# A two-layer attention kernel: moving bulk loads, small loads and a bias network to other steps

## The reference, cut to what matters

```
xn   = layernorm(x) * g_in
q    = xn @ Wq          (512 -> 16 heads x 64);   k, v = xn @ Wkv (one k and one v, shared by all heads)
k, v = a "null" key and value put ahead of the 128 keys and values
sim  = q k^T (scaled) + bias per head, causal mask, mask per item
out  = softmax(sim) v  @ Wo   (1024 -> 512)
x    = x + layernorm(out) * g_out
```

## Time and profile before

| what | us |
|---|---|
| median of 3 runs | 1381.46 |
| the three runs | 1381.04, 1381.46, 1384.83 |
| the profiled execution's own time | 1385.04 |
| its span | 1383.2 |
| PE busy in the span | 1290.3 |
| DVE, ACT, POOL busy | 1108.7, 859.8, 748.5 |
| mean granted TensorE clock | 0.973 of full speed |

### The profile page before, as it was taken

One profiled execution on the slowest core, in us unless ns is written; L12 is line 12 of the kernel. 1 busy time (PEld: TensorE's weight loads), 2 busy tenths in 40 slices (PEclk: granted clock), 3 DMA queues, 4 the chain that ended last, 5 costly groups with the idle time before them and its releaser, 6 DMA issues.

```text
span 1383.2 us, 28922 instructions
## 1 busy us (share of the span) xinstructions
PE 1290.3 (93%) x8152; PEld 1189.2 (86%) x8152; DVE 1108.7 (80%) x2968; ACT 859.8 (62%) x3245; POOL 748.5 (54%) x1337
## 2 busy tenths in 40 slices
PE   3675599999999999999989999999999999999997
PEld 3564499999999999999988899999999999999996
DVE  5573477778777877787789989999899999999886
ACT  3443366666666666666676666666666666666663
POOL 3341244444444444444446666766676667766773
PEclk8788799999999999999999999999999999999999
DMA  9106501110111111110101101110111011101101
GB/s 282 28 8 105 154 27 41 45 45 30 38 45 45 32 36 45 45 38 31 46 26 45 47 28 41 45 45 24 44 45 45 23 45 45 45 23 45 45 31 39
DMA packets 44723, 67.46 MB, mean 49 GB/s; under 512 B 8160, under 2 KB 16352, under 8 KB 44688
## 3 DMA queue, kind: packets, MB, share of 16 engines
q1 hardware_dynamic: 43056, 66.93, 16.0%
q0 software_dynamic: 288, 0.10, 0.2%
q10 hardware_dynamic: 1344, 0.02, 0.1%
HBM read 48.16 MB, written 18.87 MB: 48 GB/s over the span
## 4 chain that ended last, share of the span: by engine, by line
PE 85%; DVE 5%; SPq 4%; POOL 2%; issue 2%; ACT 1%; DMA 1%; POOLq 0%; DVEq 0%; ACTq 0%
PE bank_q L1187 27%; PE bank_y L1319 24%; PE bank_s L1187 11%; PE bank_o L1187 10%; PE bank_p L1286 6%; PE bank_t L1259 4%; PE bank_t L1227 2%; SPq L327 1%; SPq L379 1%; DMA p_sb<-in_L_cond_g 1%; PE bank_t L1264 1%; DVE wo_l L841 0%; DVE wq_l L832 0%; DVE qt_l L984 0%; DVE wq_raw L869 0%
## 5 line engine op out<-in xcount | busy, mean ns | idle before, releaser
L702 ACT ACTIVATE p_raw<-s_sb,neg_m 128x130 f32<-128x130 f32 (+1 forms) x1024 | 371.9, 366 | 144.4 <-DVE neg_m L1042 141.2
L555 POOL TENSOR_TENSOR p_sb<-p_raw,rden 128x256 f32<-128x256 f32 x256 | 157.1, 614 | 396.3 <-DVE rden L1048 396.3
L1187 PE MATMUL bank_q<-wq_h,xt_h 128*128 128x384 f32 x768 | 270.0, 352 | 7.4 <-DVE xt_l L940 7.2
L1187 PE MATMUL bank_q<-wq_h,xt_l 128*128 128x384 f32 x768 | 261.5, 340 | 0.0
L1187 PE MATMUL bank_q<-wq_l,xt_h 128*128 128x384 f32 x768 | 261.0, 340 | 0.0
L545 POOL TENSOR_TENSOR bias_g<-bias,mask_row 128x260 f32<-128x260 f32 x256 | 177.9, 695 | 125.1 <-DVE s_sb L1035 123.1
L1319 PE MATMUL bank_y<-wo_h,ot_h 128*128 128x512 f32 x512 | 218.8, 427 | 0.3 <-DVE ot_l L1058 0.3
L1319 PE MATMUL bank_y<-wo_h,ot_l 128*128 128x512 f32 x512 | 203.2, 397 | 0.0
L1319 PE MATMUL bank_y<-wo_l,ot_h 128*128 128x512 f32 x512 | 202.9, 396 | 0.0
L702 ACT ACTIVATION_READ_ACCUMULATOR p_raw<-s_sb,neg_m 128x1 f32 x1024 | 193.1, 189 | 0.0
L1035 DVE TENSOR_TENSOR s_sb<-bank_s,bias_g 128x392 f32<-128x392 f32 x256 | 143.0, 559 | 43.4 <-PE bank_s L1187 43.4
(11 more groups left out here) (124 smaller groups left out, 3113.1 us busy)
## 6 DMA issues: line engine op xcount, KB each, us to landing
x_in<-in_x SPq DMA_DIRECT2D x32, 256.0 KB, 2.7
x_res<-in_x SPq DMA_DIRECT2D x32, 256.0 KB, 2.7
x_mid<-y_out SPq DMA_DIRECT2D x32, 256.0 KB, 2.0
x_in<-x_mid SPq DMA_DIRECT2D x32, 256.0 KB, 2.7
x_res<-x_mid SPq DMA_DIRECT2D x32, 256.0 KB, 2.7
out_x<-y_out SPq DMA_DIRECT2D x32, 256.0 KB, 2.0
wq_raw<-in_L_cond_Wq SPq DMA_DIRECT2D x4, 768.0 KB, 14.2
wo_raw<-in_L_cond_Wo SPq DMA_DIRECT2D x1, 2048.0 KB, 12.9
```

The costliest lines, as they stand in the source:

```text
L555: e.tensor_tensor(to[:, 0:2 * P].rearrange("p (e j) -> p e j", e=2), low_blocks(of)[:, :, 2:LOW], r[:, 0:2, :].broadcast_to([P, 2, P]), AL ...
L702: last = e.activation(p_raw[:, g % 2, lo:hi], s_sb[:, g % 2, lo:hi], ACT.Exp, bias=neg_m[:, h:h + 1], accum_out=esum[:, h:h + 1])
L1187: last = e.matmul(out, a, b, start=(k == 0), stop=(k == len(passes) - 1))
```

## The change

In words: the loads for layer 1 leave `between(2)` and go, one group per step, into SP's step behind the load of `x_in`: the table store in step 3, Wq and Wkv in step 29, the bias reads in step 30, Wo in step 31. SP's start is put in another order (network rows ahead of the bias, the bias in two halves around `x_in` (0,1), the mask after it); the three null loads go to ACT's queue. The other small loads, with the null bias and `g_in` of layer 1 among them, are issued by POOL early (12 DMAs), followed by both `place_nulls`. ACT does one tiny exponential first. `output_weights(0, 1)` moves to step 0 on POOL and, on ACT, from behind `exps(3)` to behind `exps(2)`. On DVE and ACT the first `split_qt` stages stand ahead of the network's norm and silu. The second silu's quarters 2 and 3, the second transposes and the table move one step on (the table to the start of step 3). `net` and `net_t` move into `wq_raw`. The loops begin at item 4 instead of 3.

```
-FIRST, LAST = 3, B - 4
+FIRST, LAST = 4, B - 4
...
-        net = y_out[:, 0, :]
-        net_t = y_out[:, 1, :].rearrange("p (c t) -> p c t", c=KC)
+        net = wq_raw[:, 2, 0:D]
+        net_t = wq_raw[:, 3, 0:D].rearrange("p (c t) -> p c t", c=KC)
...
# SP
                     load_x(m)
+                if (m := at(0)) is not None:
+                    bulk(m)
...
-            def between(n):
-                if n == 2:
+            def bulk(m):
+                if is_item(m, 0, 3):
                     e.wait_ge(net_step, TABLE)
                     e.dma_start(table, table_sb.unsqueeze(1).broadcast_to([H, P, 2 * P])).then_inc(table_stored, 16)
+                if is_item(m, 0, B - 3):
                     load_wq(1)
+                if is_item(m, 0, B - 2):
+                    e.wait_ge(table_stored, 16)
+                    load_bias1()
+                if is_item(m, 0, B - 1):
                     for half in range(2):
                         e.wait_ge(wo_ready[half], 1)
                     load_wo(1)
-                    e.wait_ge(table_stored, 16)
-                    load_bias1()

             load_x((0, 0))
             load_wq(0)
-            for half in range(2):
-                rows = slice(half * DH, (half + 1) * DH)
-                null(null_k_col[rows, :], cond[0:1, :].rearrange("a d -> d a"))
-            null(null_v[:, :], cond[1:2, :].broadcast_to([P, DH]))
-            load_bias0()
-            load_mask(0)
+            for dst, src in ((w0_b, w0[0]), (b0_b, b0), (g_b[0], g0)):
+                net_row(dst, src)
+            load_bias0(0)
             wait(e, xn_ready, (0, 0))
             load_x((0, 1))
-            for dst, src in ((w0_b, w0[0]), (b0_b, b0), (g_b[0], g0)):
-                net_row(dst, src)
+            load_bias0(1)
+            load_mask(0)
             load_wo(0)
...
# POOL
+            def start_output(m):
+                if is_item(m, 0, 0):
+                    output_weights(0, 1)
             def between(n):
                 if n == 1:
-                    output_weights(0, 1)
                     net_deviation(VE2)
+                if n == 2:
                     null_norm()
-                    place_nulls(1)
...
                 on(0, normalise, 2)
+                on(0, start_output)
                 on(0, normalise, 3)
...
-            never_seen()
             causal_masks()
             inverse_deviations(item_of(-3))
+            load_small()
+            never_seen()
+            e.wait_ge(null_bias_loaded, 16 * LAYERS)
+            place_nulls(0)
+            place_nulls(1)
             mask_bias0()
             inverse_deviations(item_of(-2))
+            masked_bias((0, 0), 1)
             net_deviation(VE1)
-            e.wait_ge(null_bias_loaded, 16 * LAYERS)
-            place_nulls(0)
-            for g in (1, 0, 2):
-                masked_bias((0, 0), g)
-            load_small()
+            masked_bias((0, 0), 0)
+            masked_bias((0, 0), 2)
...
# ACT: g_in of layer 1 and the null bias go to POOL's load_small
+            load_g_in(0)
+            for half in range(2):
+                rows = slice(half * DH, (half + 1) * DH)
+                e.dma_start(null_k_col[rows, :], cond[0:1, :].rearrange("a d -> d a")).then_inc(nulls_loaded, 16)
+            e.dma_start(null_v[:, :], cond[1:2, :].broadcast_to([P, DH])).then_inc(nulls_loaded, 16)
+            e.wait_ge(consts_ready, 4)
+            e.activation(esum[:, 0:1], minus_half[:, 0:1], ACT.Exp).then_inc(act_warm, 1)
+            e.wait_ge(act_warm, 1)
...
                 on(0, exps, 2)
+                on(0, start_output, 1)
...
                 on(0, exps, 3)
-                on(0, start_output, 1)
...
-                on(1, start_copy, 2, TP2, TCOPY2)
+                on(0, start_copy, 2, TP2, TCOPY2)
...
-            net_silu(GAIN1, EXP1)
             split_qt(first, 0)
             split_qt(first, 1)
+            net_silu(GAIN1, EXP1)
...
# DVE
-                on(0, net_second_silu, [2])
...
                 on(1, split_kt)
-                on(0, net_second_silu, [3])
+                on(-1, net_second_silu, [2, 3])
...
-                if n == 2:
+                if n == 3:
                     second_null()
...
+            q_scale_out(first, 2)
             ln_apply(second)
-            q_scale_out(first, 2)
+            split_qt(first, 0)
             net_norm(RSTD1, CEN1, g_b[0])
-            split_qt(first, 0)
+            split_qt(first, 1)
             net_silu(EXP1, PLUS1, REC1, [0])
-            split_qt(first, 1)
-            net_silu(EXP1, PLUS1, REC1, [1])
             split_kt(first)
             x_stats(third)
             means_variances(item_of(-1))
-            net_silu(EXP1, PLUS1, REC1, [2, 3])
+            net_silu(EXP1, PLUS1, REC1, [1, 2, 3])
...
# PE: second transposes at item 2 instead of 1, table at item 3 instead of 2 (on DVE too)
```

More of the change, by code:

```diff
@@ L249, in build @@
         null_scaled = sem("null_scaled")
+        act_warm = sem("act_warm")
         null_col = sem("null_col")
@@ L356, in low_and_up, with load_bias0 @@
                 return low, up
-            def load_bias0():
+            def load_bias0(pair):
                 heads = bias0.rearrange("(g r e) i j -> r i g e j", g=G, r=2)
-                for pair in range(2):
-                    low, up = low_and_up(0, pair)
-                    for k in range(2):
-                        e.dma_start(low[:, :, k, :], heads[pair, HALF:P, :, k, :]).then_inc(bias0_loaded, 16)
-                        e.dma_start(up[:, :, k, :], heads[pair, 0:HALF, :, k, 0:HALF]).then_inc(bias0_loaded, 16)
+                low, up = low_and_up(0, pair)
+                for k in range(2):
+                    e.dma_start(low[:, :, k, :], heads[pair, HALF:P, :, k, :]).then_inc(bias0_loaded, 16)
+                    e.dma_start(up[:, :, k, :], heads[pair, 0:HALF, :, k, 0:HALF]).then_inc(bias0_loaded, 16)
             def load_mask(layer):
@@ L429, in _ @@
             load_mask(1)
-            stream(e, step, between)
+            stream(e, step)
             e.wait_ge(x_stored, 16 * N)
@@ L448, in load_small @@
             def load_small():
+                for layer in range(LAYERS):
+                    e.dma_start(null_bias_sb[:, layer, :], row(null_bias[layer]).broadcast_to([P, H]))\
+                        .then_inc(null_bias_loaded, 16)
                 for half in range(2):
@@ L457, in load_small @@
                 small(k_mul[:, :], row(k_scale).broadcast_to([P, DH]))
+                e.dma_start(g_in_sb[:, 1, :], g_in[1].rearrange("(c p) -> p c", p=P),
+                            allow_slow_non_contiguous=True).then_inc(g_in_loaded[1], 16)
             def null_norm():
@@ L615, in _, with load_g_in @@
         def _(e):
-            for layer in range(LAYERS):
+            def load_g_in(layer):
                 e.dma_start(g_in_sb[:, layer, :], g_in[layer].rearrange("(c p) -> p c", p=P),
-                            allow_slow_non_contiguous=True).then_inc(g_in_loaded, 16)
-            for layer in range(LAYERS):
-                e.dma_start(null_bias_sb[:, layer, :],
-                            null_bias[layer].rearrange("(a n) -> a n", a=1).broadcast_to([P, H]))\
-                    .then_inc(null_bias_loaded, 16)
+                            allow_slow_non_contiguous=True).then_inc(g_in_loaded[layer], 16)
+            load_g_in(0)
[6 more added lines that the diff above has]
+            e.wait_ge(act_warm, 1)
             def net_silu(gain, exp):
@@ L636, in project_weights @@
                 e.wait_ge(wq_loaded[p], 16 * WQ_LOADS[p] * (layer + 1))
-                e.wait_ge(g_in_loaded, 16 * LAYERS)
+                e.wait_ge(g_in_loaded[layer], 16)
                 if layer:
@@ L902, in net_table @@
             def net_table(m):
-                if is_item(m, 0, 2):
+                if is_item(m, 0, 3):
                     e.wait_ge(net_step, MM2)
```

6 lines of the change are left out of this document (2 added, 4 removed).

## The result

The changed kernel took 1340.86 us (median of four runs, 1337.61 to 1344.78); the kernel before, on the same chip, 1382.82 (1381.04 to 1384.83). The ratio is 0.9697, 95% interval 0.9663 to 0.9732: 42 us faster. The profiled execution took 1338.76 us with a span of 1337.0, 46.2 us less than the span profiled before.

What follows compares the result with a forecast made beforehand. PE, busy 93% of the span, was taken to bound the kernel, so only its idle time could be won; the terms summed to -43.7 us from 1385.04, giving 1341.3 (or 1337.8 from the median); it said 1340 us, range 1332 to 1349.

Steps and rivals of the forecast that it cites:

- The stall out of step 2, -34.2: Step 2, rid of the bulk loads, falls from 53.83 us to a steady step of 19.67: -34.2 us.
- the store in step 3, +0.3: Table store behind x_in in step 3; the next x_in lands about when x_stats wants it: +0.3 us, bounds 0 and +2.
- Layer 1's loads at steps 29 to 31, 0: Wq and Wkv, bias reads and Wo, each covered by a step of PE work: 0, bounds 0 and +5 together.
- Step 1, -11.1: Step 1 loses the wait for POOL's wo_l, half clock behind it, and the table at its end: -11.1 us, bounds -13 and -7.
- The table one step on, +6: Table chain now between steps 2 and 3, 4.8 us back plus one more reciprocal and some clock: +6 us, bounds +4 and +8.
- a little clock lost: Unpriced part of the +6 us for the table chain's new place between steps 2 and 3.
- Step 0, -5: Step 0 saves POOL's wait 2.35, wo_l's move 2.18 and clock up to 2.4, less 1.9: -5 us, bounds -7 and 0.
- The 1.9 taken off: Step 0: 1.9 us off 6.9, for PE perhaps starting at 1.2 GHz and POOL's wo_l running beside DVE's.
- The start, +0.3: Ahead of step 0, split_xt at about 39.1 against 38.87, set by x_in of (0,2): +0.3 us, bounds -1.5 and +3.
- the main case: The summed forecast holds, 1335 to 1345 us by its own bounds; chance 0.60.
- start and step 0 give nothing: Rival: small loads and wo_l on POOL beside DVE's weight splits lose the -5, start costs +3; 1349 us, chance 0.17.
- More is won: Rival: start wins 1.5, step 0 gives -7, step 1 -13, the table costs 4; 1333.6, from the median 1330; chance 0.12.

Runs made afterwards that it cites:

- the undoing run: Changed kernel with the network's second silu, transposes and table put back one step, table ahead of step 2; 1343.18 us, ratio 0.9697.
- the repeat: The changed kernel measured once more with no edit, on another chip; 1342.94 us, ratio 0.9693.

## Why the prediction was right, and where by luck

The forecast was 1340; the median is 1340.86. Its steps, one by one:

- **The stall out of step 2, -34.2, and the store in step 3, +0.3: right and shown.** Done alone they give -35.2 by the medians (-33.9 foreseen), and the step falls to 19.73 us. The landing of `x_in` behind the table was foreseen within a microsecond of what `x_stats` wants; it waits 0.73 us there. The slow side of this mechanism is shown as well, by Wq behind the store.
- **Layer 1's loads at steps 29 to 31, 0: right.** The margins were larger than the prediction's bound from the table's pace feared; even all in one step cost nothing. `wq_h` is first made at 649.51, 14.9 us behind the issue at 634.63, with Wq landed after 6.0 to 7.8.
- **Step 1, -11.1: right.** The step lost 11.6 us. Of it 5.0 are shown by putting `wo_l` back, where the sum had 6.6 (5.5 of wait, 1.1 of clock), and 4.8 by putting the chain back, where it had 4.5; no run was made for the other 1.8.
- **The table one step on, +6: right in kind and size.** Step 2 stands 5.5 us above a steady step, and the undoing run confirms that the gain in step 1 and this loss cancel. What the prediction called "a little clock lost" is 0 in some executions and 2.7 to 2.8 us in others.
- **Step 0, -5: right in sum, its terms not.** From `split_xt` to the next `transpose_x` the kernel before took 30.62 us, and 28.98 in the profile of the bulk loads alone; the changed program took 24.9 to 26.6. The 2.18 for `wo_l`'s move is shown (2.1 by its undoing). The 2.35 for POOL's wait is the wait of one execution: 1.26 stood there in the profile of the bulk loads alone, and putting the nine loads back brought 0.80. The 2.4 for the clock was too much: at a granted 1.00 the product takes 3.70 us, 1.24 less than 4.94, since in the kernel before only its first half ran at half the clock. The 1.9 taken off made up for it. Of the two costs that it stood for, PE did begin the step at half the clock (0.50 from 41 to 43 us), as it had in the kernel before; the other, POOL's and DVE's `wo_l` side by side, never came: DVE's `wo_l` ran at 57.26, behind the end of POOL's at 55.98, and took 2.48 us for four, and `split_v` had run at 45.62 in 0.36, ahead of POOL's. The port rule of the Trainium skill (SBUF — State Buffer, the two sides) is not tested by step 0, as the instructions never met; the 1.66 us of `split_v` in the run with Wo put back agree with it. But there `split_v` was through at 76.67, while POOL's four instructions ran until 77.80: it was not held up by all that was left of the four, as the prediction had it for DVE's `wo_l`.
- **The start, +0.3: the term that was mis-sized, and hidden by the first profile.** There `split_xt` came at 39.03 as foreseen (39.1), and for the reason given, `x_in` of (0,2). But over eight profiles of that start it stands at 38.36 to 41.02, mean 39.9, and in the two with the old start at 38.87 and 37.03. In seven of the eight the only transfer that DVE waits for behind `x_in` of (0,1) is the mask, which the change puts behind `x_in` (0,1) and the second half of the bias. The prediction did write that "the mask and the second half of the bias land later than before" and then gave it no price of its own; the bound of +3, which was meant for the twelve small loads, holds it. The difference of the means is 2.0 us, from few profiles of a start that varies by itself. The mask's place alone isn't shown to cost that: with SP's old order in the changed kernel `split_xt` came at 39.28, behind two other late transfers.

Set against the execution it was made for, the sum of -43.7 stands beside -46.2 in span: 2.5 us too little, half to 0.8 of a microsecond in each of four places (start and step 0, step 1, step 2, the rest). The median was hit more closely because the first profile is itself 2.1 us below the changed kernel's median. And by medians, what the change does beyond the bulk loads was priced at -9.8; measured it is the gain of the whole less that of the bulk loads alone, each against the kernel before on its own chip: 42.0 - 35.2 = 6.8 us, or 41.7 - 35.2 = 6.5 by the repeat. The start's 1.7 over its term and the clock behind the chain are of the right size for the difference. The traces say the same of start and step 0 taken together: `transpose_x` of (0,2), their end, stood at 69.49 and 66.01 with the old start and at 63.23 to 67.12, mean 65.1, in the seven profiles of programs that leave both as the change made them. That is 2.6 us by the means, where the sum had 4.7 and the first profile showed 5.6. And 1340 itself was a choice between 1341.3 and 1337.8, according to whether the 3.58 us that the profiled execution had over the median would go; no run tells. Nor does the main case's "1335 to 1345" follow from its bounds: added up they give 1333 to 1362. So the agreement within 1 us is partly luck; the mechanisms and the signs are not.

The rival "start and step 0 give nothing" falls by its time of 1349 and by the waits that went in step 0, but it was nearer than the first profile says: about half of what was priced there came. "More is won" was not what happened, but its number was within reach: another place for the chain and the start give 1332.3.

What stays open: why the mask lands at 22.8 in one execution and at 25.5 in the next, and why the same idle time sometimes costs the clock. The nine small loads' worth rests on one trace, since 1.3 us lies inside the spread of the times. So does what start and step 0 gain, on two profiles of the old start; and 1.8 us of step 1 have no run of their own.

## What to carry to other kernels

In the one queue of this kernel the place of a transfer counted more than its size: look at what stands ahead of the load that the next step wants, and move the slow one (here a store of 22.4 us) behind it, with a full step of cover. An ordered chain across engines that is moved one step on keeps its stall; it goes when each link has its own gap, on the engine that feeds the others too. And at a start with several late transfers, removing one wait gives nothing until the next late one is moved with it (0.5 us for the first, 3.0 to 3.9 for the second here): list all of them before judging an edit.

## What was not expected of the hardware

- The same idle time of PE (1.67 and 1.68 us busy in a window of 4) left the granted clock at 1.00 once, while it stood at 0.50 behind it the other time, and the next step took 19.64 or 22.20 us. A term for the clock behind this wait of some 2.5 us is a range, 0 to 2.8 us, not a number.
- Issuing three Wq loads takes SP 1.52 us in step 29, with nothing large ahead of them, and 16.67 to 17.41 us behind the table's store: the wait shows as the length of the issue, not as idle time.
- The same start differs by 2.7 us over eight profiles, all of it ahead of `split_xt` (two executions of one program differ by 2.0), while 1165.3 to 1168.1 us pass from `transpose_x` of (0,7) to the end of the span in all fourteen profiles of this study, in twelve of them 1165.3 to 1166.6.
